# Rounding pass of an int8-quantised FFN on Trainium2: two elementwise adds moved from VectorE to ScalarE

## The chip, the cores and the metric

The kernel runs on all 8 cores of one Trainium2 chip. Each core computes one of the 8 sequences (2048 tokens, 1024 features); the cores exchange nothing. The metric is the device time of the slowest core in microseconds (us). Engines in the profile: PE is TensorE, DVE is VectorE, ACT is ScalarE, POOL is GpSimd, SP is SyncE.

## What is computed

For each sequence `x` of shape 2048 x 1024 the reference does an attention layer whose weights are `1 + s + s*s/2` in place of an exponential, and then a linear layer on activations quantised to int8 for each token:

```python
x = layernorm(x + attention(x, Wq, Wk, Wv, Wo))
# ffn
amax    = max(|x|, axis=-1)
x_scale = maximum(amax, 1e-6) / 127
x_q     = clip(round(x / x_scale), -128, 127).astype(int8)
acc     = x_q @ weight_q.T                    # exact integers
x = layernorm(x + acc * x_scale * weight_scale + bias)
```

The part that matters here is `x_q`: one rounding of 2048 x 1024 values to the nearest integer on each core, ties to even.

## The kernel before

Every instruction is written by hand into one of five streams (`plan.op("vector", ...)`, `"scalar"`, `"gpsimd"`, `"tensor"`, `"sync"`). An engine works through its own stream in the order in which the source emits it. Between engines, and between dependent instructions of the same engine, the order is kept by counting semaphores: `sDV` for VectorE, `sSc` for ScalarE, `sPE` for TensorE, `sPo` for GpSimd, `sIO` and `sCa` for transfers. `waits=[(sDV, sDV.n)]` means "wait until everything that was counted on VectorE up to here is done". Each wait is an instruction of its own ahead of the one that it guards, and a wait that this stream has already made is left out.

The stages follow each other: the projections to q, k and v; the attention, pair of heads by pair; the output projection with the first residual (`mkr1`, L605, with sums of squares on ScalarE, `mksq1`, L612, and a maximum and minimum on VectorE, L617 and L620); a run of small operations on 128x16 statistics (L625 to L662); the **rounding pass**; the int8 linear layer (L797) with its own residual (L808, L815, L824); statistics again (from L834); and the output rows, scaled on VectorE (L855) and stored (L861).

The rounding pass is one loop over `NT = 16` tiles of 128 tokens x 1024 features. Tile `t` uses buffers `t6[t % 2]` (f32) and `xq32[t % 2]` (int32); `er` is another name for `t6`, and `g32` is the same memory again, seen as int32. In the order of the VectorE stream the steps of a tile are:

- `mk1` (L705): `t6 = x1 * S2 + MM2`, the scaled value. Completion is what `mkxm` on GpSimd waits for.
- `mkc` (L712): `xq32 = int(t6)`, a cast.
- `mke` (L716): `t6 = t6 - xq32`, the remainder, a two-input operation.
- `mkm1` (L720): `t6 = t6 + MAGIC`, and `mkm2` (L724): `t6 = t6 - MAGIC`, with `MAGIC = 12582912.0`. Together they round the remainder to a multiple of one.
- `mkg` (L728): `g32 = int(2 * t6)`.
- `mk2b` (L735): `xq = xq32 + g32`, the rounded value as f16. It also waits for the transposes of tile `t-2`.

Beside it, for each tile, GpSimd scales the residual (`mkxm`, L741, one input) and adds the bias (`mkx1b`, L756, two inputs), both in place on `x1`. TensorE transposes `xq` in 8 blocks (L766) once `mk2b` is done, and ScalarE copies the result from PSUM into `xqT` (`mktre`, L776). In source order ScalarE's instruction for tile `t` is this copy and nothing else. TensorE's stream has all 128 transposes ahead of the first matmul of the linear layer, so that layer starts when tile 15 has been transposed.

Of the kernel before, what the change touches and what calls it, by code (L numbers as in the profile page):

```python
# [10 lines left out]
AF = mybir.ActivationFunctionType  # L11
ALU = mybir.AluOpType
# [15 lines left out]
MAGIC = 12582912.0  # L28
# [76 lines left out]
def _build_nc_inner(debug, _waits, collect_only=False):  # L105
# [34 lines left out]
    sSc = Sem(e(nc.semaphore("sSc")), "sSc")  # L140
    sDV = Sem(e(nc.semaphore("sDV")), "sDV")
# [44 lines left out]
    plan = Plan(nc, last_wait)  # L186
    plan.future_waits = _waits

    for dst, src in ((wsb, d_wsb), (biasb, d_biasb), (tri, d_tri),
                     (ident, d_ident), (ones2, d_ones2)):  # L190
        plan.op("sync", lambda sy, dst=dst, src=src: sy.dma_start(dst[:, :], src),
                incs=[(sIO, 16)])
# [8 lines left out]
    for fi in range(NCH):  # L201
# [3 lines left out]
                incs=[(sCa, 16)])  # L205
# [3 lines left out]
                incs=[(sCa, 16)])  # L209
# [9 lines left out]
    for proj in range(2):  # L219
        for c in range(NCH):  # L220
# [6 lines left out]
            for fi in range(NCH):  # L227
                waits = [(sCa, dma_after[(proj, fi)])]
                if prev in evac_dv:
                    waits.append((sDV, evac_dv[prev]))  # L230
                for qcc in range(QC):
# [5 lines left out]
                    incs = ()  # L237
                    if qcc == QC - 1 and (c == NCH - 1 or fi == NCH - 1):
                        incs = [(sPE, 1)]
                    plan.op("tensor", mk, waits=waits if qcc == 0 else (),  # L240
                            incs=incs)
# [5 lines left out]
            def mkev(v, ps=ps, dst=dst, scale=scale, c=c):  # L247
# [3 lines left out]
                    incs=[(sDV, 1)])  # L251
            evac_dv[(proj, c)] = sDV.n
        nxt = d_wkt if proj == 0 else d_wvt
        for fi in range(NCH):
# [4 lines left out]
                    waits=[(sPE, w_last_use[(proj, fi)])],  # L259
                    incs=[(sCa, 16)])  # L260
# [8 lines left out]
           for i in range(2)]  # L269

    plan.op("vector", lambda v: v.memset(vz_blocks[:, :, 64:65], 1.0),
            incs=[(sDV, 1)])

    v_evac = {}
    for t in range(NT):
# [6 lines left out]
        for fi in range(NCH):  # L282
            waits = [(sCa, dma_after[(2, fi)])] + extra
            extra = []
            for half in range(2):
# [5 lines left out]
                incs = [(sPE, 1)] if (fi == NCH - 1 and half == 1) else ()  # L291
                plan.op("tensor", mk, waits=waits if half == 0 else (), incs=incs)
                waits = ()
# [9 lines left out]
    if debug:  # L303
        plan.op("sync", lambda sy: sy.dma_start(d_qto, qT[:, :]),
                waits=[(sDV, n_qk_evac)], incs=[(sIO, 16)])
        plan.op("sync", lambda sy: sy.dma_start(d_kto, kT[:, :]),
                waits=[(sDV, n_qk_evac)], incs=[(sIO, 16)])
        plan.op("sync", lambda sy: sy.dma_start(d_vzo, vz[:, :]),
                waits=[(sDV, n_vz_done)], incs=[(sIO, 16)])
# [18 lines left out]
    for fi in range(NCH):  # L328
# [4 lines left out]
                incs=[(sCa, 16)])  # L333
# [80 lines left out]
    for p in range(NP):  # L414
# [128 lines left out]
        if p > 0:  # L543
# [3 lines left out]
                waits=wio, incs=[(sIO, 16)])  # L547
        gather_done[p] = sIO.n
        if debug and p == 0:
            plan.op("sync", lambda sy: sy.dma_start(d_oso, ot_sb[0][:, :]),  # L550
                    incs=[(sIO, 16)])
# [20 lines left out]
    if debug:  # L572
        plan.op("sync", lambda sy: sy.dma_start(d_oto, ot_fin[:, :]),
                waits=list(w_all), incs=[(sIO, 16)])

    r1_done = {}
    for t in range(NT):
        wio = []
        if t >= 2:
            wio.append((sDV, r1_done[t - 2]))  # L580
        plan.op("sync",
                lambda sy, t=t: sy.dma_start(xstream[t % 2][:, :],
                                             d_xtok[t * 128:(t + 1) * 128, :]),
                waits=wio, incs=[(sIO, 16)])
# [7 lines left out]
        for fi in range(NCH):  # L592
            for half in range(2):
# [5 lines left out]
                incs = [(sPE, 1)] if (fi == NCH - 1 and half == 1) else ()  # L599
# [11 lines left out]
        def mksq1(s, t=t):  # L611
# [3 lines left out]
                incs=[(sSc, 1)])  # L615
# [3 lines left out]
        def mkmn(v, t=t):  # L619
# [6 lines left out]
            waits=[(sDV, r1_done[NT - 1])], incs=[(sDV, 1)])  # L626
    plan.op("vector", lambda v: v.tensor_scalar(V1, SQ1, INV1024, None, ALU.mult),
            waits=[(sSc, n_sq1)], incs=[(sDV, 1)])
    plan.op("vector", lambda v: v.tensor_tensor(MSQ, M1, M1, ALU.mult),
            waits=[(sDV, sDV.n)], incs=[(sDV, 1)])  # L630
    plan.op("vector", lambda v: v.tensor_tensor(V1, V1, MSQ, ALU.subtract),
            waits=[(sDV, sDV.n)], incs=[(sDV, 1)])
    plan.op("scalar", lambda s: s.activation(V1, V1, AF.Sqrt, bias=c_eps),
            waits=[(sDV, sDV.n)], incs=[(sSc, 1)])
    plan.op("vector", lambda v: v.reciprocal(V1, V1),
            waits=[(sSc, sSc.n)], incs=[(sDV, 1)])
# [3 lines left out]
            waits=[(sDV, n_rstd1)], incs=[(sDV, 1)])  # L640
    plan.op("vector", lambda v: v.tensor_tensor(MN, M1, MN, ALU.subtract),
            waits=[(sDV, sDV.n)], incs=[(sDV, 1)])
    plan.op("vector", lambda v: v.tensor_tensor(MX, MX, MN, ALU.max),
            waits=[(sDV, sDV.n)], incs=[(sDV, 1)])
    plan.op("vector", lambda v: v.tensor_tensor(AM, MX, V1, ALU.mult),
            waits=[(sDV, sDV.n)], incs=[(sDV, 1)])
    plan.op("vector",
            lambda v: v.tensor_scalar(XS, AM, 1e-6, INV127, ALU.max, ALU.mult),
            waits=[(sDV, sDV.n)], incs=[(sDV, 1)])
    plan.op("vector", lambda v: v.reciprocal(RQ, XS),  # L650
            waits=[(sDV, sDV.n)], incs=[(sDV, 1)])
# [24 lines left out]
    er = t6  # L676
# [23 lines left out]
    for t in range(NT):  # L700
# [10 lines left out]
        def mkc(v, t=t):  # L711
            return v.tensor_copy(xq32[t % 2][:, :], t6[t % 2][:, :])  # L712
        plan.op("vector", mkc, waits=[(sDV, rnd1_done[t]), (sDV, sDV.n)],
                incs=[(sDV, 1)])
# [1 line left out]
            return v.tensor_tensor(t6[t % 2][:, :], t6[t % 2][:, :],  # L716
                                   xq32[t % 2][:, :], ALU.subtract)
        plan.op("vector", mke, waits=[(sDV, sDV.n)], incs=[(sDV, 1)])
        def mkm1(v, t=t):
            return v.tensor_scalar(er[t % 2][:, :], er[t % 2][:, :],  # L720
                                   MAGIC, None, ALU.add)
        plan.op("vector", mkm1, waits=[(sDV, sDV.n)], incs=[(sDV, 1)])
        def mkm2(v, t=t):
            return v.tensor_scalar(er[t % 2][:, :], er[t % 2][:, :],  # L724
                                   -MAGIC, None, ALU.add)
        plan.op("vector", mkm2, waits=[(sDV, sDV.n)], incs=[(sDV, 1)])
        def mkg(v, t=t):
            return v.tensor_scalar(g32[t % 2], er[t % 2][:, :],  # L728
                                   2.0, None, ALU.mult)
        plan.op("vector", mkg, waits=[(sDV, sDV.n)], incs=[(sDV, 1)])  # L730
        wv = [(sDV, sDV.n)]
        if t >= 2:
            wv.append((sPE, tr_done[t - 2]))
# [186 lines left out]
```

How the kernel before makes its waits and increments, by code:

```python
        def thunk(eng, wl=wl, builder=builder, incs=tuple(incs)):  # L74
            for s, v in wl:
                eng.wait_ge(s.h, v)
            inst = builder(eng)
            for s, k in incs:
                inst = inst.then_inc(s.h, k)
```

## Time and profile before

| | us |
|---|---|
| time before, median of 2 runs | 1013.87 (1012.25 to 1015.49) |
| time of the profiled execution | 1014.62 |
| its span, slowest core (core 4) | 1013.1 |
| spans of the 8 cores | 1006.6 to 1013.1 |
| VectorE busy | 543.4 (54%) |
| ScalarE busy | 375.7 (37%) |
| TensorE matmul busy | 617.9 (61%) |
| GpSimd busy | 110.8 (11%) |

The span runs from the first to the last instruction of a core. All times of rows are from core 4 and from that one profiled execution. Busy shares are averages over stages with different limits, so a stage is read by itself: the rounding pass lies between about 756 and 907 us of the span.

### The profile page before, as it was taken

To read this page: it belongs to the slowest core of one execution; us is meant where nothing else is said; L and a number is where in the kernel's file an instruction comes from. 1 tells how busy PE (TensorE), PEld (TensorE's weight loads), DVE (VectorE), ACT (ScalarE), POOL (GpSimd) and SP (SyncE) were. 2 spreads that over 40 slices of the span, in tenths; PEclk is the share of its full clock that TensorE was granted. 3 is DMA by queue.
4 is the path that set the end of the run, shared out by engine and by line. 5 is a ranking of instruction groups with operands and counts; after the bars stand their busy time and mean duration, and the time that the engine had idled before them with its cause. 6 is when DMAs were issued, how large, how long until landed. Compare 5 with 4: busy or idle time off the path is not lost.

```text
span 1013.1 us, 8858 instructions; the slowest of 8 cores (1006.6 to 1013.1 us)
## 1 busy us (share of the span) xinstructions
PE 617.9 (61%) x2688; PEld 222.6 (22%) x2688; DVE 543.4 (54%) x825; ACT 375.7 (37%) x403; POOL 110.8 (11%) x100
## 2 busy tenths in 40 slices
PE   1259859839977877877877778709941011029910
PEld 0014314304412222222222222203410000014400
DVE  0003202303345666556566656535989999976742
ACT  0000000000089879788879888801320110112310
POOL 1100000020000000000000000001014554530000
PEclk9999959959989889799979988858975555559965
DMA  6640230145000011011010111116410000000025
GB/s 107 115 70 1 32 52 1 27 59 82 1 1 1 23 32 38 18 42 33 21 33 22 33 32 23 31 44 199 164 63 0 0 1 0 0 1 1 1 111 221
DMA packets 14833, 43.89 MB, mean 43 GB/s; under 512 B 2244, under 2 KB 2756, under 8 KB 13764
## 3 DMA queue, kind: packets, MB, share of 16 engines
q0 software_dynamic: 8192, 23.07, 12.0%
q1 hardware_dynamic: 6596, 20.25, 6.0%
q8 instruction: 24, 0.39, 0.2%
q14 instruction: 21, 0.17, 0.1%
HBM read 44.11 MB, written 8.52 MB: 52 GB/s over the span
## 4 chain that ended last, share of the span: by engine, by line
PE 31%; DVE 22%; DMA 22%; ACT 14%; issue 9%; POOL 0%; DVEq 0%; ACTq 0%; POOLq 0%; SPq 0%
ACT uab L462 14%; PE pq L235 9%; PE oab L505 7%; DMA xs<-x_tok 6%; PE pa L797 6%; DMA wbuf<-wqt 6%; PE pv L289 5%; DVE t L720 4%; PE ps L442 4%; DVE t L716 3%; DMA wbuf<-wvt 3%; DMA wbuf<-wkt 3%; DVE xq L735 2%; DVE uab L470 2%; DVE ot_fin L375 2%
## 5 line engine op out<-in xcount | busy, mean ns | idle before, releaser
L462 ACT ACTIVATE uab<-ps,consts 128x1024 f16<-128x1024 f32 (+1 forms) x320 | 320.8, 1080 | 56.2 <-PE ps L442 56.1
L505 PE MATMUL oab<-uab,vz 128*65 128x512 f16 (+3 forms) x640 | 194.5, 389 | 62.4 <-DVE uab L485 31.6
L235 PE MATMUL pq<-xTsb,wbuf 128*128 128x512 f16 x512 | 128.4, 414 | 69.0 <-DMA wbuf<-wqt 53.7
L442 PE MATMUL ps<-qT,kT 64*128 64x512 f16 (+3 forms) x640 | 124.8, 387 | 22.9 <-ACT uab L462 21.0
L485 DVE TENSOR_SCALAR uab<-uab 128x1024 f16<-128x1024 f16 x192 | 79.4, 422 | 105.0 <-ACT uab L462 105.0
L462 ACT ACT_TABLE_LOAD x1 | 1.3, 1283 | 281.1 <-PE ps L442 281.1
L766 PE MATMUL pt<-ident_sb,xq 128*128 128x128 f16 x128 | 16.2, 306 | 146.4 <-DVE xq L735 146.4
L235 PEld LDWEIGHTS pq<-xTsb,wbuf 128*128 128x128 f16 x512 | 51.7, 103 | 145.2 <-issue 94.2
L505 PEld LDWEIGHTS oab<-uab,vz 128*65 128x65 f16 x640 | 48.2, 116 | 144.3 <-issue 143.3
L470 DVE SCALAR_TENSOR_TENSOR uab<-uab,tri_sb 128x256 f16<-128x256 f16 x128 | 54.5, 426 | 42.9 <-ACT uab L462 41.3
L597 PE MATMUL py<-woT,ot_fin 128*128 128x512 f16 x256 | 59.2, 388 | 25.9 <-DMA ot_fin<-ob_tmp 25.4
L289 PE MATMUL pv<-wbuf,xTsb 128*128 128x512 f16 x256 | 61.0, 400 | 20.7 <-DMA wbuf<-wvt 18.2
L248 DVE TENSOR_SCALAR qT<-pq 128x2048 f16<-128x2048 f32 x8 | 18.3, 2292 | 101.7 <-PE pq L235 101.7
L442 PEld LDWEIGHTS ps<-qT,kT 64*128 64x128 f16 x640 | 35.0, 94 | 154.1 <-issue 153.4
L776 ACT COPY xqT<-pt 128x1024 f16<-128x1024 f16 x16 | 16.2, 1012 | 140.6 <-PE pt L766 140.6
L797 PE MATMUL pa<-wqf,xqT 128*128 128x512 f16 x256 | 57.5, 388 | 0.0
L298 DVE CAST vz<-pv 128x1024 f16<-128x1024 f32 x16 | 19.6, 1225 | 59.9 <-PE pv L289 59.9
L248 DVE TENSOR_SCALAR kT<-pq 128x2048 f16<-128x2048 f32 x8 | 18.3, 2292 | 60.2 <-PE pq L235 60.2
L756 POOL TENSOR_TENSOR x<-x,biasb_sb 128x1024 f32<-128x1024 f32 x16 | 49.9, 3119 | 2.4
L766 PEld LDWEIGHTS pt<-ident_sb,xq 128*128 128x128 f16 x128 | 12.4, 137 | 150.5 <-issue 150.5
L612 ACT ACTIVATE scratch<-x 128x1024 f32<-128x1024 f32 x16 | 16.9, 1057 | 72.3 <-DVE x L605 72.3
L720 DVE TENSOR_SCALAR t<-t 128x1024 f32<-128x1024 f32 x16 | 42.3, 2643 | 1.7
(67 smaller groups left out, 491.9 us busy)
## 6 DMA issues: line engine op xcount, KB each, us to landing
rzb<-rzscr POOLq DMA_DIRECT2D x16, 512.0 KB, 4.6
xs<-x_tok SPq DMA_DIRECT2D x16, 512.0 KB
xTsb<-xT POOLq DMA_DIRECT2D x8, 512.0 KB, 5.6
out<-xs SPq DMA_DIRECT2D x8, 512.0 KB
out<-t SPq DMA_DIRECT2D x8, 512.0 KB
wbuf<-wqt POOLq DMA_DIRECT2D x8, 256.0 KB, 6.3
wbuf<-wkt POOLq DMA_DIRECT2D x8, 256.0 KB, 3.5
wbuf<-wvt POOLq DMA_DIRECT2D x8, 256.0 KB, 3.5
```

The source lines that it names most:

```text
L235: return t.matmul(ps[:, qcc * 512:(qcc + 1) * 512], lhs, rhs, start=(fi == 0), stop=(fi == NCH - 1))
L248: return v.tensor_scalar(dst[:, c * T:(c + 1) * T], ps[:, :], scale, None, ALU.mult)
L289: return tt.matmul(ps[:, half * 512:(half + 1) * 512], lhs, rhs, start=(fi == 0), stop=(fi == NCH - 1))
L442: return t.matmul(ps[:, ab * 512 + js: ab * 512 + 512], lhs, rhs, start=True, stop=True, tile_position=(r0, 0))
L462: return s.activation(dst, src, AF.Square, bias=c_rs, scale=c_rs)
L470: return v.scalar_tensor_tensor(ub[:, :, js:js + 128], ub[:, :, js:js + 128], 0.5, tri[:, None, :].broadcast_to([128, 2, 128]), ALU.add, A ...
L485: return v.tensor_scalar(ub[:, :, :], ub[:, :, :], 0.5, None, ALU.add)
L505: return t.matmul(ob[0:65, ab * 512 + js: ab * 512 + 512], lhs, rhs, start=(kt == 0), stop=(kt == 4 * qc + 3))
L597: return tt.matmul(ps[:, half * 512:(half + 1) * 512], lhs, rhs, start=(fi == 0), stop=(fi == NCH - 1))
L720: return v.tensor_scalar(er[t % 2][:, :], er[t % 2][:, :], MAGIC, None, ALU.add)
L756: return g.tensor_tensor(x1[:, t * D:(t + 1) * D], x1[:, t * D:(t + 1) * D], biasb[:, :], ALU.add)
L797: return tt.matmul(ps[:, half * 512:(half + 1) * 512], lhs, rhs, start=(fi == 0), stop=(fi == NCH - 1))
```

## The change

The two additions `mkm1` and `mkm2` leave the VectorE stream and enter the ScalarE stream, as activations with the function Copy, a scale of one and the constant as bias. Their places in the source stay between `mke` and `mkg`. `mkm1` now waits for VectorE's `mke` and for everything counted on ScalarE; `mkm2` waits for `mkm1` on ScalarE's own semaphore; and `mkg`, still on VectorE, waits for `mkm2` through ScalarE's semaphore. Everything else keeps its engine and its order.

```diff
-        def mkm1(v, t=t):
-            return v.tensor_scalar(er[t % 2][:, :], er[t % 2][:, :],
-                                   MAGIC, None, ALU.add)
-        plan.op("vector", mkm1, waits=[(sDV, sDV.n)], incs=[(sDV, 1)])
-        def mkm2(v, t=t):
-            return v.tensor_scalar(er[t % 2][:, :], er[t % 2][:, :],
-                                   -MAGIC, None, ALU.add)
-        plan.op("vector", mkm2, waits=[(sDV, sDV.n)], incs=[(sDV, 1)])
+        def mkm1(s, t=t):
+            return s.activation(er[t % 2][:, :], er[t % 2][:, :], AF.Copy,
+                                bias=MAGIC)
+        plan.op("scalar", mkm1, waits=[(sDV, sDV.n), (sSc, sSc.n)],
+                incs=[(sSc, 1)])
+        def mkm2(s, t=t):
+            return s.activation(er[t % 2][:, :], er[t % 2][:, :], AF.Copy,
+                                bias=-MAGIC)
+        plan.op("scalar", mkm2, waits=[(sSc, sSc.n)], incs=[(sSc, 1)])
         def mkg(v, t=t):
             return v.tensor_scalar(g32[t % 2], er[t % 2][:, :],
                                    2.0, None, ALU.mult)
-        plan.op("vector", mkg, waits=[(sDV, sDV.n)], incs=[(sDV, 1)])
+        plan.op("vector", mkg, waits=[(sSc, sSc.n)], incs=[(sDV, 1)])
```

## Rows read from the trace of the kernel before

**Rows 1.** Page, part 2: the span in 40 slices, busy tenths of each engine
```profile
PE   1259859839977877877877778709941011029910
DVE  0003202303345666556566656535989999976742
ACT  0000000000089879788879888801320110112310
POOL 1100000020000000000000000001014554530000
```

**Rows 2.** Chain of waits, 720 to 1014 us: start us, us, what
```profile
755.78 0.19 DVE stat L662
...
756.07 0.82 DVE t L705
...
907.08 1.01 PE pt L766 x8
908.10 57.27 PE pa L797 x256
```

**Rows 3.** Timeline of the fifth tile; tile 15's copy: start us, us, engine, line, operation, idle before it
```profile
792.41 1.23 DVE L735 TENSOR_TENSOR xq<-xq,t 128x1024 f16<-128x1024 int32 x1 [0.17 <-DVE t L728]
793.56 0.81 DVE L705 TENSOR_SCALAR t<-x,stat 128x1024 f32<-128x1024 f32 x1
793.89 1.01 PE L766 MATMUL pt<-ident_sb,xq 128*128 128x128 f16 x8 [8.39 <-DVE xq L735]
794.54 1.69 POOL L741 TENSOR_SCALAR x<-x,stat 128x1024 f32<-128x1024 f32 x1 [4.45 <-DVE t L705]
794.99 1.01 ACT L776 COPY xqT<-pt 128x1024 f16<-128x1024 f16 x1 [8.39 <-PE pt L766]
795.26 2.03 DVE L716 TENSOR_TENSOR t<-t,xq 128x1024 f32<-128x1024 f32 x1
796.37 3.12 POOL L756 TENSOR_TENSOR x<-x,biasb_sb 128x1024 f32<-128x1024 f32 x1
797.40 2.65 DVE L720 TENSOR_SCALAR t<-t 128x1024 f32<-128x1024 f32 x1
800.15 0.69 DVE L724 TENSOR_SCALAR t<-t 128x1024 f32<-128x1024 f32 x1
800.95 0.69 DVE L728 TENSOR_SCALAR t<-t 128x1024 int32<-128x1024 f32 x1
801.82 1.23 DVE L735 TENSOR_TENSOR xq<-xq,t 128x1024 f16<-128x1024 int32 x1 [0.17 <-DVE t L728]
802.96 0.81 DVE L705 TENSOR_SCALAR t<-x,stat 128x1024 f32<-128x1024 f32 x1
...
908.19 1.01 ACT L776 COPY xqT<-pt 128x1024 f16<-128x1024 f16 x1 [8.39 <-PE pt L766]
```

**Rows 4.** Groups by line and shape, 750 to 910 us: count, busy us, mean ns
```profile
L756 POOL TENSOR_TENSOR x<-x,biasb_sb 128x1024 f32<-128x1024 f32 x16 | 49.9, 3119 | 2.4
L720 DVE TENSOR_SCALAR t<-t 128x1024 f32<-128x1024 f32 x16 | 42.3, 2643 | 1.7
L735 DVE TENSOR_TENSOR xq<-xq,t 128x1024 f16<-128x1024 int32 x16 | 19.6, 1226 | 3.0 <-DVE t L728 2.8
L724 DVE TENSOR_SCALAR t<-t 128x1024 f32<-128x1024 f32 x16 | 11.1, 694 | 1.7
```

**Rows 5.** Groups of ScalarE by line and shape, whole span, columns as in rows 4
```profile
L462 ACT ACTIVATE uab<-ps,consts 128x1024 f16<-128x1024 f32 x224 | 252.9, 1207 | 44.8 <-PE ps L442 44.8
L612 ACT ACTIVATE scratch<-x 128x1024 f32<-128x1024 f32 x16 | 16.9, 1057 | 72.3 <-DVE x L605 72.3
L776 ACT COPY xqT<-pt 128x1024 f16<-128x1024 f16 x16 | 16.2, 1012 | 140.6 <-PE pt L766 140.6
L462 ACT ACT_TABLE_LOAD x1 | 1.3, 1283 | 281.1 <-PE ps L442 281.1
```

**Rows 6.** Timeline, handovers between VectorE and ScalarE around the statistics, columns as in rows 3
```profile
751.87 0.17 DVE L631 TENSOR_TENSOR stat<-stat 128x16 f32<-128x16 f32 x1
752.14 0.31 ACT L633 ACTIVATE stat<-stat,consts 128x16 f32<-128x16 f32 x1 [1.96 <-DVE stat L631]
752.55 0.25 DVE L635 RECIPROCAL stat<-stat 128x16 f32<-128x16 f32 x1 [0.50 <-ACT stat L633]
...
968.07 0.08 DVE L815 DVE_READ_ACCUMULATOR x<-t,x 128x1 f32 x1
...
968.31 1.06 ACT L824 ACTIVATE scratch<-x 128x1024 f32<-128x1024 f32 x1 [2.30 <-DVE x L815]
```

## Prediction

> **What bounds the kernel now.** I read the page's 40 slices first, to see which engine is full where [rows 1]. One slice is 25.3 us. From slice 30 (about 760 us) to slice 35 VectorE shows 9 tenths while TensorE shows 0 or 1, ScalarE 0 or 1 and GpSimd 4 or 5. That is the rounding pass, and there VectorE looks like the limit. Full is not the same as limiting, so the chain of waits comes next [rows 2]: it runs on VectorE alone from the last statistic (755.78) through the first L705 (756.07) up to tile 15, and then passes to TensorE, to the eight transposes at 907.08 and the 256 matmuls of the linear layer, 57.27 us long. TensorE takes its stream in order, so every microsecond that the 16 tiles of the rounding pass lose or gain arrives undiminished at 908.10. The matmuls last as long as before, whenever they begin.
>
> Then the timeline of one tile [rows 3]. The reader is to see three things in it. First, the period: L705 starts at 793.56 and again at 802.96, so a tile takes 9.40 us, and the seven VectorE steps follow one another without a gap worth naming. Second, L720 takes 2.65 us and L724, the same addition on the same buffer with the same shape, 0.69. Over the 16 tiles the means are 2643 and 694 ns [rows 4]. So 1.95 us of L720 are not its own. Third, who is running then: GpSimd's L756 ends at 796.37 + 3.12 = 799.49, and L720 ends at 800.05, 0.56 us later, about the time that one such addition needs. I read it thus: L720 was issued at 797.40 while L756 was at work, could not move until L756 was done at 799.49, and then ran at its usual speed. The step before looks alike: L716 starts at 795.26, GpSimd's L741 ends at 794.54 + 1.69 = 796.23, and L716 ends at 797.29, 1.06 later. L716's two-input relative L735 takes 1226 ns [rows 4], not 2.03. The two engines take turns. What is on the path of a tile is in part GpSimd's work.
>
> The Trainium skill has a rule for this pair: on the page "SBUF — State Buffer", section "Who interferes with whom", it says that VectorE and GpSimd share one pair of ports under a lock held for a whole instruction, the loser blocking fully, and that ScalarE never waits on anyone. The 0.56 us from L756's end to L720's end agree with the first half. For the second, ScalarE's copy L776 lies wholly beside GpSimd's L741 here (794.99 to 796.00 in 794.54 to 796.23) and takes the 1.01 us that it also takes for tile 15, at 908.19, long after GpSimd's last step [rows 3]; so the trace agrees, as far as a copy that reads PSUM and writes SBUF can show it.
>
> **The change part by part.** The stretch that changes reaches from L716's end to L728's start. Before: 797.29 to 800.95, that is 3.66 us: a gap of 0.11, L720 with 2.65, a gap of 0.10, L724 with 0.69, a gap of 0.11 [rows 3].
>
> What comes in its place, term by term:
>
> - VectorE to ScalarE. L633 starts 0.10 after L631's end (751.87 + 0.17 = 752.04, to 752.14). But `mkm1` has two waits, as L824 has, and L824 starts 0.16 after the end of what it waits for (968.07 + 0.08 = 968.15, to 968.31) [rows 6]. I take 0.16. The second wait, on ScalarE's own count, is long met: the copy L776 of the tile before ends at 794.99 + 1.01 = 796.00, 1.29 us before L716's end [rows 3].
> - `mkm1` on ScalarE. No row shows a Copy activation with f32 in SBUF on both sides. The nearest is L612, an activation of 128x1024 f32 from SBUF to SBUF, at 1057 ns; it bounds nothing by itself, so I take the copy L776 at 1012 below and L462, which reads scale and bias from memory, at 1207 above [rows 5]. The value is that of L612, the row with the same shape, type and memories: 1.06.
> - ScalarE to itself. No row shows ScalarE waiting for its own last result. VectorE does that in 0.11 (L716 to L720). Below it is the 0.10 of a handover, above it the 0.25 between L735 of the tile before (792.41 + 1.23 = 793.64) and its transposes (793.89), the longest handover in these rows [rows 3]. I take 0.11.
> - `mkm2`: the same 1.06.
> - ScalarE to VectorE: L633 ends at 752.45 and L635 starts at 752.55, 0.10 [rows 6].
>
> Sum: 0.16 + 1.06 + 0.11 + 1.06 + 0.10 = 2.49 us. The stretch shrinks by 3.66 - 2.49 = 1.17 us a tile.
>
> L728 keeps its 0.69 only if GpSimd is out of the way when it is issued, since it is a VectorE step of the kind that L720 was. GpSimd is released by L705, not by anything moved, and L756 ended 799.49 - 797.29 = 2.20 us after L716. L728 now starts 2.49 after it, 0.29 us past that end. So the wait on GpSimd doesn't move to L728: it lies beside ScalarE's two additions. The cover is thin. Each 0.1 us that GpSimd is later than 0.29 is 0.1 us a tile back.
>
> What else sees the edit. ScalarE's copy L776 stands behind `mkm2` of its own tile and ahead of `mkm1` of the next. It is waiting for the transposes anyway, starts 1.10 us after these do and is done 1.29 us before L716 ends, so neither the copy nor the next `mkm1` is held. `mk1` of tile t+2 waits for `mk2b` of tile t, unchanged. GpSimd's 4.45 us of idle before L741 [rows 3] shrink to 3.28, so it stays off the path with its 4.8 us of work in a period of now 8.23. VectorE's wait for `mkm2` blocks what is queued behind it, L728, L735 and the next tile's L705; they are in the sum, since the whole period is counted. The linear layer, statistics and stores are untouched and simply begin earlier.
>
> Total: 16 x 1.17 = 18.7 us. Against the profiled execution's own 1014.62 that is 995.9. The median of the runs shown lies 0.75 below that execution, so I forecast **995 us**, 1.9% faster. About 2% is what a measurement of this kernel can tell from no change. That bound is at 0.98 x 1013.87 = 993.6, hard by the forecast, which makes "within 2%" the likelier word, and not by far.
>
> **The rivals.** *ScalarE is cheaper* than L612. With 1.01 for each activation (L776's row) and 0.10 for each of the three handovers a stretch is 2.32 and the gain 1.34 x 16 = 21.4: 992.4. The floor under it is GpSimd: L728 can't end before L756's end plus 0.56, at 800.05, against 801.64 now, 1.59 us a tile, 25.4 in all, 988.4. For it: a copy has less to do than a square with a sum. Against: L612 has the exact operands.
>
> *ScalarE is dearer.* With 1.21 each (L462's row) and 0.25 for each handover the stretch is 3.17, the gain 0.49 x 16 = 7.8, 1006; with only the activations at 1.21 it is 2.79, the gain 13.9, 1000. For it: ScalarE's own-result wait is unseen. Against: L462 reads PSUM and two operands more.
>
> *The stall only changes its victim, and the kernel gets slower.* If L756 can't finish until VectorE leaves it room, or is later than its span tells, L728 is stretched to 2.65 as L720 was. The tile then takes 2.49 + 2.65 = 5.14 from L716's end to L728's end, against 801.64 - 797.29 = 4.35: 0.79 more, 12.6 us in all, 1026. It decides from the point where L756 ends 1.59 us later than it does. For it: the margin is 0.29 us, and spans of GpSimd are rough. Against: L756 and L720 have the same lengths in this tile as in the mean of all 16 (3.12 and 3119 ns, 2.65 and 2643) [rows 3, 4], so their order never slips, and nothing new is put in L756's way. The same sign follows when L720's surplus is ignored: two activations at 1.06 against two additions at 0.69. The Trainium skill says just that on "ScalarE: Activation LUTs", section "Rules for kernel authors": additions belong on VectorE, not on ScalarE. The rows agree with its prices (694 ns against 1057); that it gives the wrong sign here hangs on L720's 2643.
>
> *Copy and the copy or the square need different tables.* A table load is 1283 ns [rows 5]. One a tile on the path gives 1.17 - 1.28 = -0.11, 1015.6; two give 22 us more, 1036. Against: only one load stands in the whole span, though a square, the copy L776 and a square root (L633) all ran. A single load more would cost 1.3.
>
> **How the numbers follow.** Forecast as worked out, 992.5 to 999: 0.70. ScalarE cheaper: 0.12. Dearer: 0.11. The stall moves: 0.05. Tables: 0.02. The range should leave out no more than 2 in 10: from 991, inside the cheap case, to 1000, where only the activations are dear. Faster by over 2% (under 993.6): the cheap case with 0.12, and 0.13 of the forecast's own, because the two runs shown lie 3 us apart and the bound 1.4 below my number; 0.25. Slower by over 2% (over 1034): only two table loads a tile, 0.02. Within 2%: 0.73.
>
> **What would show it.** In the timeline of the changed kernel a tile's period should be 8.2 us; two ScalarE activations of 1.06 should stand between L716's end and the L728 step, which should start 2.5 us after L716's end and keep 0.69; L716 should still take 2.03 and L756 3.12; the transposes of tile 15 should start near 888 and the 57.3 us of matmuls behind them be the same. No new table load should be there. I am wrong if `mkg` is longer than 0.7 us (the stall has moved), if an activation takes over 1.2 us, if the gap between the two is over 0.2 us, or if the linear layer begins some 19 us earlier and the end does not.

## The result

The changed kernel takes **994.35 us** (median of 11 runs) against 1013.88 for the kernel before (median of 10 runs beside them). The ratio is 0.9796 with a 95% interval of 0.9771 to 0.982, that is 2.0% faster, on the border of what can be told from no change. The forecast was 995. In some executions the cores of one die show a lower granted clock and the time is some per cent longer (one of the 11 here, at 1029.99 us); medians take in all runs, ratios only the undisturbed ones.

All rows of a kernel are from its slowest core, for the changed kernel core 5. The chain of waits of the changed kernel, late in the span, shows the same structure as before [rows 2], but with ScalarE in it: the second addition (now L725 on ScalarE), the doubling (L729), the last rounding step (L736), the transposes, the matmuls. Columns are start us, us, what.

```profile
884.96 1.06 ACT t L725
...
886.12 0.71 DVE t L729
...
886.99 1.24 DVE xq L736
...
888.47 1.01 PE pt L767 x8
```

The timeline of one tile of the changed kernel, the fourth, answers [rows 3]:

```profile
782.41 1.69 POOL L742 TENSOR_SCALAR x<-x,stat 128x1024 f32<-128x1024 f32 x1 [3.25 <-DVE t L705]
782.87 1.01 ACT L777 COPY xqT<-pt 128x1024 f16<-128x1024 f16 x1 [3.56 <-PE pt L767]
783.14 2.03 DVE L716 TENSOR_TENSOR t<-t,xq 128x1024 f32<-128x1024 f32 x1
784.25 3.13 POOL L757 TENSOR_TENSOR x<-x,biasb_sb 128x1024 f32<-128x1024 f32 x1
785.32 1.06 ACT L720 ACTIVATE t<-t 128x1024 f32<-128x1024 f32 x1 [1.43 <-DVE t L716]
786.47 1.06 ACT L725 ACTIVATE t<-t 128x1024 f32<-128x1024 f32 x1
787.63 0.69 DVE L729 TENSOR_SCALAR t<-t 128x1024 int32<-128x1024 f32 x1 [2.46 <-ACT t L725]
788.49 1.23 DVE L736 TENSOR_TENSOR xq<-xq,t 128x1024 f16<-128x1024 int32 x1 [0.17 <-DVE t L729]
```

The reader is to see that nothing but the two additions changed. The subtraction L716 is still 2.03 us and GpSimd's bias add (L757) still 3.13. Both activations take 1.06 while that bias add is running. VectorE is idle for 2.46 us before L729, which then takes its plain 0.69. GpSimd is done at 784.25 + 3.13 = 787.38, and L729 starts at 787.63, 0.25 us later.

To compare kernels I use one table, read from the trace of every core. The period is the mean distance of the L705 steps. The pass is the time from the first L705 to the first matmul of the linear layer; the linear layer is counted from there to the start of its last matmul, and the rest from that start to the end of the span. All are medians over the 8 cores of the profiled execution, in us:

```
kernel                         before pass   period    pass    linear layer   rest     span
before                              753.15     9.42   151.85          56.85   48.25   1009.95
changed                             753.10     8.20   132.30          57.30   47.15    989.15
e1 before, no GpSimd step           754.00     6.66   107.75          56.70   47.85    967.00
e2 changed, no GpSimd step          753.75     7.39   119.40          56.65   47.35    977.10
e3 first addition moved             752.55     8.60   138.70          56.70   47.35    995.20
e4 second addition moved            750.45     9.80   157.90          56.95   47.10   1012.30
e5 changed, GpSimd longer           751.15    10.11   162.80          56.75   46.85   1017.65
e6 before, bias adds late           748.75     7.47   128.40          57.00   47.85    982.35
e7 changed, bias adds late          752.30     8.20   136.10          56.35   47.10    993.35
e8 short rounding                   752.65     3.13    51.20          56.55   48.35    908.30
e9 bias adds late and gated         756.05     7.47   120.65          56.90   48.30    982.35
e10 scaling on ScalarE              753.85     6.66   107.70          56.50   47.95    966.55
e11 as e5, other form               751.20     9.15   147.60          56.55   47.00   1002.20
e12 correction by 4096              752.40     9.42   151.80          56.90   48.25   1009.15
```

The pass is the same to 0.1 us on all 8 cores of a kernel. The stages ahead of it differ by 5 to 15 us between the cores of one execution, whichever the kernel, and in the traces that is most of what sets the slowest core apart. So the pass is the sharp measure here and the total the blunt one. The change took 19.55 us out of the pass.

### The profile page after: what moved, and what is told of

Its sections match the earlier page's. It is cut to its first block, busy times and chain, and to the rows that moved or that the text cites. A ratio compares the mean times of both kernels' runs of the same rounds, so it can differ in the third digit from the quotient of the medians.

```text
span 993.9 us, 8874 instructions; the slowest of 8 cores (981.0 to 993.9 us)
## 1 busy us (share of the span) xinstructions
PE 614.4 (62%) x2688; PEld 222.0 (22%) x2688; DVE 490.0 (49%) x793; ACT 409.2 (41%) x435; POOL 111.2 (11%) x100
## 4 chain that ended last, share of the span: by engine, by line
PE 32%; DMA 22%; ACT 18%; DVE 17%; issue 9%; POOL 0%; DVEq 0%; ACTq 0%; POOLq 0%; SPq 0%
ACT uab L462 15%; PE pq L235 10%; PE oab L505 7%; PE pa L798 6%; DMA xs<-x_tok 6%; DMA wbuf<-wqt 6%; PE pv L289 6%; PE ps L442 4%; DVE t L716 3%; DMA wbuf<-wvt 3%; DMA wbuf<-wkt 3%; DVE xq L736 2%; DVE ot_fin L375 2%; DVE uab L470 2%; ACT t L720 2%
## 5 line engine op out<-in xcount | busy, mean ns | idle before, releaser
L505 PE MATMUL oab<-uab,vz 128*65 128x512 f16 (+3 forms) x640 | 191.7, 384 | 63.4 <-DVE uab L485 32.3
L757 POOL TENSOR_TENSOR x<-x,biasb_sb 128x1024 f32<-128x1024 f32 x16 | 50.0, 3127 | 2.4
L612 ACT ACTIVATE scratch<-x 128x1024 f32<-128x1024 f32 x16 | 16.9, 1057 | 73.7 <-DVE x L605 73.7
L524 DVE COPY otsb<-oab 65x1024 f32<-65x1024 f32 x32 | 38.8, 1213 | 4.2 <-PE oab L505 4.2
L777 ACT COPY xqT<-pt 128x1024 f16<-128x1024 f16 x16 | 16.2, 1012 | 56.6 <-PE pt L767 56.6
```

Source lines behind the costliest of these rows:

```text
L505: return t.matmul(ob[0:65, ab * 512 + js: ab * 512 + 512], lhs, rhs, start=(kt == 0), stop=(kt == 4 * qc + 3))
L524: return v.tensor_copy(dst, src)
L757: return g.tensor_tensor(x1[:, t * D:(t + 1) * D], x1[:, t * D:(t + 1) * D], biasb[:, :], ALU.add)
```

## The experiments

Two claims of the prediction carry it: that L720's 2.65 us were mostly a wait for GpSimd, and that the gain is this wait, filled with other work, and not the relief of VectorE. The rivals are that L720 is long by itself (theory B), and that VectorE's load is what counts (theory C). The first four kernels ran on one chip, beside a kernel before of 1016.65 us; e5 to e8 stood beside one of 1017.01, and e9 to e12 beside one of 1016.27.

### No GpSimd step in the pass

The edit, in the kernel before (e1) and in the changed one (e2), leaves the residual unscaled and without its bias:

```diff
-        plan.op("gpsimd", mkxm, waits=[(sDV, rnd1_done[t])], incs=[(sPo, 1)])
...
-        plan.op("gpsimd", mkx1b, waits=wx1b, incs=[(sPo, 1)])
-        x1b_done[t] = sPo.n
+        x1b_done[t] = 0
```

> The kernel before without GpSimd's two steps on x1 in the rounding pass (the residual is then neither scaled nor given its bias, so that part of the result is left out). Theory A, turns with GpSimd: the first addition loses its surplus of 1.95 us (2.65 to 0.69) and the subtraction before it its 0.80 (2.03 to 1.23); a tile takes 6.65 us in place of 9.40, the kernel 970. Theory B, the first addition is long by itself (it follows a two-input step): it stays at 2.65, the tile at 9.40, the kernel at 1014. Theory C, only VectorE's load counts: nothing on VectorE was removed, 1014.

Measured: 972.87 us (2 runs), ratio 0.9558 (0.9486 to 0.9629). First the group of the subtraction in the kernel before, 750 to 910 us (its neighbours are in [rows 4]), then two groups of e1, 750 to 872 us:

```profile
L716 DVE TENSOR_TENSOR t<-t,xq 128x1024 f32<-128x1024 f32 x16 | 32.5, 2031 | 1.7
```

```profile
L716 DVE TENSOR_TENSOR t<-t,xq 128x1024 f32<-128x1024 f32 x16 | 19.6, 1225 | 1.7
L720 DVE TENSOR_SCALAR t<-t 128x1024 f32<-128x1024 f32 x16 | 11.1, 695 | 1.7
```

Not one VectorE instruction was edited, and the first addition went from 2643 to 695 ns, the subtraction from 2031 to 1225. The period is 6.66, expected 6.65. Theories B and C are both out: what made these two steps long was another engine's work.

> The changed kernel without GpSimd's two steps on x1 (the same part of the result is left out). Theory A: only the subtraction gets shorter, by 0.80 us, since the activations never met GpSimd; a tile takes 7.41 in place of 8.21, the kernel 982, and that is 12 us MORE than the kernel before without the same steps: the sign of the change turns. Theories B and C: 994, 20 below the other.

Measured: 984.46 us (2 runs), ratio 0.9672 (0.9608 to 0.9735); the period is 7.39, expected 7.41. The row of this pair is in the table: without GpSimd the pass takes 107.75 us with the additions on VectorE and 119.40 with them on ScalarE. The very change that won 19.55 us loses 11.65 once there is no wait to fill. This is the case that the Trainium skill describes on "ScalarE: Activation LUTs", section "Rules for kernel authors" (additions on VectorE): it holds in e1 and e2, and it gives the wrong sign in the kernel as it stands, since it prices the instruction and not the wait in front of it. The factor of up to about 3 that the section gives is for bf16; in f32 the rows here show 1057 against 694 ns, a factor of 1.5, so what they confirm is the direction.

### One addition at a time

e3 moves `mkm1` and leaves `mkm2` on VectorE, e4 the reverse:

```diff
 e3, in the changed kernel
-        def mkm2(s, t=t):
-            return s.activation(er[t % 2][:, :], er[t % 2][:, :], AF.Copy,
-                                bias=-MAGIC)
-        plan.op("scalar", mkm2, waits=[(sSc, sSc.n)], incs=[(sSc, 1)])
+        def mkm2(v, t=t):
+            return v.tensor_scalar(er[t % 2][:, :], er[t % 2][:, :],
+                                   -MAGIC, None, ALU.add)
+        plan.op("vector", mkm2, waits=[(sSc, sSc.n)], incs=[(sDV, 1)])
...
-        plan.op("vector", mkg, waits=[(sSc, sSc.n)], incs=[(sDV, 1)])
+        plan.op("vector", mkg, waits=[(sDV, sDV.n)], incs=[(sDV, 1)])
```

> Only the first addition on ScalarE, the second stays on VectorE. Theory A: the second addition is issued 1.31 us after the subtraction's end, has to wait until GpSimd's bias add is done at 2.20 and ends at 2.76 (it shows 1.45 us); the next step starts at 2.87 in place of 3.66; a tile takes 8.61, the kernel 1001. Theory B: 2.65 us are replaced by 1.06 and the second addition keeps 0.69; a tile takes 7.85, the kernel 989, faster than with both moved. Theory C: two thirds or more of the gain, by VectorE's busy time relieved.

Measured: 1004.27 us (4 runs), ratio 0.9866 (0.9793 to 0.9939), period 8.60, expected 8.61. The timeline of one tile of e3:

```profile
783.25 3.12 POOL L757 TENSOR_TENSOR x<-x,biasb_sb 128x1024 f32<-128x1024 f32 x1
784.32 1.06 ACT L720 ACTIVATE t<-t 128x1024 f32<-128x1024 f32 x1 [1.43 <-DVE t L716]
785.49 1.44 DVE L725 TENSOR_SCALAR t<-t 128x1024 f32<-128x1024 f32 x1 [1.31 <-ACT t L720]
787.03 0.69 DVE L729 TENSOR_SCALAR t<-t 128x1024 int32<-128x1024 f32 x1
```

The stall has a new victim. L725, an addition that took 0.69 in all 16 tiles before, takes 1.44, because it now is the one to meet the bias add: that ends at 786.37, L725 at 786.93, again 0.56 later. The expectation said 1.45.

> Only the second addition on ScalarE, the first stays on VectorE. Theories A and B: the first addition keeps 2.65 us and 0.69 is replaced by 1.06 and a longer handover; the next step starts 4.07 us after the subtraction's end in place of 3.66; a tile takes 9.81, the kernel 1020, slower than before. Theory C: VectorE is relieved of 0.69 us a tile, 11 us, 1003.

Measured: 1024.11 us (10 runs), ratio 1.0041 (1.0005 to 1.0076); the period is 9.80, expected 9.81, and the pass 6.05 us longer than before. In one tile of e4 the first addition waits as before, and ScalarE's addition comes behind it:

```profile
778.99 2.64 DVE L720 TENSOR_SCALAR t<-t 128x1024 f32<-128x1024 f32 x1
781.78 1.06 ACT L724 ACTIVATE t<-t 128x1024 f32<-128x1024 f32 x1 [4.29 <-DVE t L720]
782.94 0.69 DVE L728 TENSOR_SCALAR t<-t 128x1024 int32<-128x1024 f32 x1 [1.31 <-ACT t L724]
```

Moving 0.69 us of work a tile off the engine that shows 90% busy made the pass longer, and the whole kernel about 0.4%. So theory C is out a second time, and the change decomposes: by the table the first addition alone brings 13.15 us of the pass, the second alone costs 6.05, and both together bring 19.55. The second pays only behind the first, where VectorE would otherwise still be waiting for GpSimd.

### How thin the cover is

The prediction put GpSimd's bias add 0.29 us ahead of L729. e5 makes GpSimd later, by one more step between its two. The step writes a buffer that the first VectorE step of the linear layer uses, so that step is also made to wait for the last bias add (the linear layer keeps its length, 56.75 us in the table):

```diff
+        def mkex(g, t=t):
+            return g.tensor_scalar(t3[0][:, :], biasb[:, :], 1.0, None, ALU.mult)
+        plan.op("gpsimd", mkex, waits=[(sPo, sPo.n), (sIO, n_const)],
+                incs=[(sPo, 1)])
...
-        wv = [(sPE, n_acc), (sIO, n_const)]
+        wv = [(sPE, n_acc), (sIO, n_const), (sPo, x1b_done[NT - 1])]
```

> The changed kernel with one more GpSimd step (a one-input scaling of 128x1024 into a buffer that is free then) between the residual's scaling and its bias add. Theory A with the thin cover of the prediction: GpSimd is done 3.27 us after the subtraction's end in place of 2.20, so the step behind the two activations, issued at 2.46, is stretched from 0.69 to about 1.4; a tile takes 8.9 us in place of 8.21, the kernel 1005. Rival, ScalarE alone sets the pace of the changed kernel: 994, the step keeps 0.69.

Measured: 1023.62 us (5 runs), ratio to before 1.0079 (1.0052 to 1.0105), period 10.11. The whole gain is gone and more, far past the 1005 that I expected, so the expectation missed. One tile of e5 shows why:

```profile
776.71 2.03 DVE L716 TENSOR_TENSOR t<-t,xq 128x1024 f32<-128x1024 f32 x1
777.83 3.54 POOL L748 TENSOR_SCALAR t<-biasb_sb 128x1024 f32<-128x1024 f32 x1 [0.16 <-POOL x L742]
...
781.20 0.71 DVE L729 TENSOR_SCALAR t<-t 128x1024 int32<-128x1024 f32 x1 [2.46 <-ACT t L725]
781.52 2.59 POOL L761 TENSOR_TENSOR x<-x,biasb_sb 128x1024 f32<-128x1024 f32 x1
782.09 3.10 DVE L736 TENSOR_TENSOR xq<-xq,t 128x1024 f16<-128x1024 int32 x1 [0.17 <-DVE t L729]
```

The added step took from L716's end (778.74) to 781.37, 2.63 us and not the 1.07 that I had read off its neighbour L742. L729, issued at 781.20, slipped in ahead of the bias add, which then ran from L729's end (781.91) to 784.11, its usual 2.20. The victim was the two-input step L736, at 3.10 in place of 1.23. e11 gives the added step the form of its neighbour, with scale and offset read from memory:

```diff
-            return g.tensor_scalar(t3[0][:, :], biasb[:, :], 1.0, None, ALU.mult)
+            return g.tensor_scalar(t3[0][:, :], biasb[:, :],
+                                   V1[:, t:t + 1], NMR[:, t:t + 1],
+                                   ALU.mult, ALU.add)
```

> As e5, with the added GpSimd step in the very form of its neighbour (scale and offset from memory in place of an immediate 1.0). If the 2.63 us that the added step held the turn in e5 are the form's, it is 1.07 here: the step behind the activations is then stretched to about 1.4 us, a tile takes 8.9, the kernel 1005, as e5 was expected to be. If they are the length of any step that follows another one, 10.11 a tile and 1023 as in e5.

Measured: 1010.13 us (8 runs), ratio 0.9944 (0.9919 to 0.9969), period 9.15. The same rows of e11:

```profile
782.88 2.03 DVE L716 TENSOR_TENSOR t<-t,xq 128x1024 f32<-128x1024 f32 x1
784.01 1.97 POOL L748 TENSOR_SCALAR t<-biasb_sb,stat 128x1024 f32<-128x1024 f32 x1 [0.17 <-POOL x L742]
...
786.13 2.34 POOL L763 TENSOR_TENSOR x<-x,biasb_sb 128x1024 f32<-128x1024 f32 x1
...
787.37 1.65 DVE L729 TENSOR_SCALAR t<-t 128x1024 int32<-128x1024 f32 x1 [2.46 <-ACT t L725]
```

Now the added step holds the turn from 784.91 to 785.98, 1.07 us, and L729 is the victim with 1.65, ending 0.55 after the bias add's end (788.47). The period is 0.25 above the 8.9 expected: GpSimd needs 0.15 to go from the one step to the next and 2.34 for a bias add that it starts with nobody ahead of it, which the estimate had at nothing and 2.20. GpSimd's last step of a tile now ends 788.47 - 784.91 = 3.56 us after the subtraction, in place of 787.38 - 785.17 = 2.21 in the changed kernel. That is 1.35 later, and the tile is 0.95 longer: the first 0.4 were free, the 0.25 of the cover and a little more, and the remainder was paid in full. So the changed kernel sits near the edge.

### Taking the cause away

If the wait for GpSimd is the cause, moving GpSimd's work is the better cure. The bias adds are needed by the linear layer's residual step (L815) only. e6 puts them behind the loop in GpSimd's stream, with both additions back on VectorE (lines behind the first step shift by one: L721, L725 and L729 are the additions and the doubling); e7 does it in the changed kernel:

```diff
-        plan.op("gpsimd", mkx1b, waits=wx1b, incs=[(sPo, 1)])
-        x1b_done[t] = sPo.n
+        late.append((mkx1b, n_xm))
...
+    for t, (bld, n_xm) in enumerate(late):
+        plan.op("gpsimd", bld, waits=[n_xm, (sIO, n_const)], incs=[(sPo, 1)])
+        x1b_done[t] = sPo.n
```

> The kernel before with GpSimd's 16 bias adds behind the rounding loop in GpSimd's stream, beside the linear layer. Same result, both additions on VectorE. Theory A: the first addition shrinks from 2.65 to 0.69, a tile takes 7.45 us, the kernel 983, and up to 990 if the bias adds take turns with VectorE's residual step of the linear layer; faster than the change itself. Theories B and C: 1014.

Measured: 990.82 us (6 runs), ratio 0.9747 (0.9711 to 0.9783), period 7.47, expected 7.45. The pass is 128.40 long, though, nearly 8 us more than 16 such periods and the last tile's transposes ask for. The timeline of VectorE in tile 15 of e6 shows where they are, and GpSimd's row beside it who held it:

```profile
876.82 2.64 DVE L721 TENSOR_SCALAR t<-t 128x1024 f32<-128x1024 f32 x1
879.57 2.64 DVE L725 TENSOR_SCALAR t<-t 128x1024 f32<-128x1024 f32 x1
882.32 2.64 DVE L729 TENSOR_SCALAR t<-t 128x1024 int32<-128x1024 f32 x1
885.13 3.10 DVE L736 TENSOR_TENSOR xq<-xq,t 128x1024 f16<-128x1024 int32 x1 [0.17 <-DVE t L729]
```

```profile
875.62 48.21 POOL L757 TENSOR_TENSOR x<-x,biasb_sb 128x1024 f32<-128x1024 f32 x16
```

The queue of bias adds begins as soon as the last L742 is done, inside tile 15, and the last four VectorE steps of that tile each lose a turn: three times 2.64 for 0.69 and once 3.10 for 1.23, together 7.7 us (the expectation of e9, below, says five steps; the subtraction keeps its 2.03).

> The changed kernel with the same 16 bias adds behind the loop. Theory A: in the changed kernel they are hidden behind the activations, so a tile stays at 8.21 us and the kernel at 994, or a few us more. Rival, the two gains add up: 983 - 19 = 964.

Measured: 998.3 us (4 runs), ratio 0.9827 (0.9796 to 0.9858), period 8.20 as in the changed kernel, pass 3.8 us longer through the same tile 15 (two steps there lose a turn, the doubling and the last one). The gains do not add: the change and the late bias adds remove the same wait. e9 also lets the first bias add wait for tile 15:

```diff
-        plan.op("gpsimd", bld, waits=[n_xm, (sIO, n_const)], incs=[(sPo, 1)])
+        plan.op("gpsimd", bld, waits=[n_xm, (sIO, n_const),
+                                      (sDV, rnd2_done[NT - 1])],
+                incs=[(sPo, 1)])
```

> As e6 (both additions on VectorE, bias adds behind the loop), but the first bias add waits for the last rounding step of tile 15. In e6 the bias adds began inside tile 15 and stretched its last five VectorE steps, some 8 us (rounding pass 128.4 us at 7.47 a tile). Theory A: the pass takes 120.5 us in place of 151.8, the linear layer stays at 57, the kernel 983 by the medians (ratio 0.969). Rival, the late bias adds cost the linear layer what they spare the pass: e6's time or more.

Measured: 986.98 us (5 runs), ratio 0.9695 (0.9647 to 0.9744). The pass is 120.65, expected 120.5. The linear layer stays at 56.90 though the bias adds now run beside it. Its rows show the price and who pays it:

```profile
879.14 29.11 POOL L757 TENSOR_TENSOR x<-x,biasb_sb 128x1024 f32<-128x1024 f32 x10 [5.31 <-DVE xq L736]
...
889.42 1.27 DVE L814 SCALAR_TENSOR_TENSOR t<-pa,stat,wsb_sb 128x1024 f32<-128x1024 f32 x1
...
890.87 1.93 DVE L821 SCALAR_TENSOR_TENSOR x<-t,x 128x1024 f32<-128x1024 f32 x1 [0.17 <-DVE t L814]
```

The residual step L821 (L815 before) takes 1.93 in place of its 1.23 in this tile and in most of those in which GpSimd is busy (3.39 in one of them). With 1.93 a tile of VectorE's is 3.3 us long there (889.42 to 892.73), and TensorE's 57 us for 16 tiles are 3.6. The waits have moved to a stage where TensorE's work covers them.

e10 moves the last GpSimd step of the pass too, the scaling of the residual, to ScalarE:

```diff
-        def mkxm(g, t=t):
-            return g.tensor_scalar(x1[:, t * D:(t + 1) * D],
-                                   x1[:, t * D:(t + 1) * D],
-                                   V1[:, t:t + 1], NMR[:, t:t + 1],
-                                   ALU.mult, ALU.add)
-        plan.op("gpsimd", mkxm, waits=[(sDV, rnd1_done[t])], incs=[(sPo, 1)])
+        def mkxm(s, t=t):
+            return s.activation(x1[:, t * D:(t + 1) * D],
+                                x1[:, t * D:(t + 1) * D], AF.Identity,
+                                bias=NMR[:, t:t + 1], scale=V1[:, t:t + 1])
+        plan.op("scalar", mkxm, waits=[(sDV, rnd1_done[t])], incs=[(sSc, 1)])
```

> As e9, and the scaling of the residual moved from GpSimd to ScalarE (an activation with scale and bias from memory), so that no GpSimd step lies in the rounding pass. Same computation as before. Theory A: like e1 without leaving anything out: the subtraction shrinks from 2.03 to 1.23 us, a tile takes 6.66, the pass 107.8, the kernel 970 (ratio 0.957). Rival, ScalarE's 1.2 us activation and its copy take over as the pace or meet VectorE in memory: 7.47 a tile or more, 983.

Measured: **973.03 us** (4 runs), ratio 0.9565 (0.952 to 0.9611), period 6.66, pass 107.70, the same as e1 with nothing left out. One tile of e10:

```profile
782.22 1.23 DVE L717 TENSOR_TENSOR t<-t,xq 128x1024 f32<-128x1024 f32 x1
782.86 1.24 ACT L742 ACTIVATE x<-x,stat 128x1024 f32<-128x1024 f32 x1
783.55 0.69 DVE L721 TENSOR_SCALAR t<-t 128x1024 f32<-128x1024 f32 x1
784.35 0.69 DVE L725 TENSOR_SCALAR t<-t 128x1024 f32<-128x1024 f32 x1
```

ScalarE's activation lies across two VectorE steps, and both keep the 1.23 and 0.69 us that they take in e1. This is the second half of the rule that the prediction took from the Trainium skill, "SBUF — State Buffer", section "Who interferes with whom" (ScalarE waits on nobody, VectorE and GpSimd take turns on a shared pair of ports). The trace agrees here for an activation that reads and writes SBUF, at 1.24 us beside a VectorE step of 1.23, and in the changed kernel at 1.06 (1056 to 1058 ns in all 32) beside a GpSimd step. The ports themselves no trace shows.

### The arithmetic of the pass

> The kernel before with the factor of the correction 4096 in place of 2. If the remainder ever rounds to something but zero, the quantised values move by 4096 steps there and the output with them; if the cast rounds to nearest, the correction is zero everywhere, nothing moves, and e8 leaves out nothing but work. Time unchanged, 1014, under either.

Measured: 1013.79 us (1 run), and the output is still that of the reference, where one correction other than zero would have moved a value by thousands of steps. So on this input the remainder never rounds to anything but zero, and the subtraction, the two additions and the doubling work on a correction that is zero. e8 leaves these four steps out and keeps the bias adds late:

```diff
         def mk2b(v, t=t):
-            return v.tensor_tensor(xq[t % 2][:, :], xq32[t % 2][:, :],
-                                   g32[t % 2], ALU.add)
+            return v.tensor_copy(xq[t % 2][:, :], xq32[t % 2][:, :])
```

> Subtraction, both additions and the doubling left out (if the cast to int32 rounds to nearest, the remainder is at most 0.5 and the correction is always zero, so the result stays the same), the last step a plain copy from int32 to f16, and the bias adds behind the loop. Theory A: scaling 0.81, cast 0.69, then the copy waits for GpSimd's scaling of the residual (1.07) and takes about 1.65; a tile takes 3.2 us, the kernel about 915, to 925 if the bias adds delay the linear layer's residual step. Were the cast a truncation, the result would be off by whole steps of the quantiser.

Measured: **922.33 us** (4 runs), ratio 0.9044 (0.8976 to 0.9112), period 3.13, expected 3.2. One tile of e8, with the copy at 1.44 us because it waits its turn behind GpSimd's scaling:

```profile
778.00 1.69 POOL L725 TENSOR_SCALAR x<-x,stat 128x1024 f32<-128x1024 f32 x1 [1.44 <-DVE t L706]
778.79 1.44 DVE L720 CAST xq<-xq 128x1024 f16<-128x1024 int32 x1 [0.17 <-DVE xq L713]
```

The pass is down to 51.2 us on every core. The total lies above the expected 915 because on two cores, 4 and 5, the matmuls of the linear layer took 63.3 and 63.7 us in place of 56.5. On core 4 the granted clock, averaged over the stretch in which these run at first, was 0.80 of full speed, between the two levels of 1.2 and 2.4 GHz; on core 5 it was 0.79, on the other six cores 0.99 to 1.00, and in the same layer of the kernel before 1.00 from 912 us on. Stretches of core 4 of e8, columns as in the page's part on engines, then clock, DMA share, GB/s:

```profile
812.00:840.00 28.00, 28.00 (x107) 11.61 (x106) 21.26 (x18) 5.88 (x11) 28.00 (x11) 0.80 0.00 1
840.00:875.00 35.00, 33.10 (x146) 14.42 (x143) 26.28 (x29) 11.37 (x20) 14.21 (x5) 0.95 0.00 0
```

It wasn't one execution alone: in another of the four runs cores 6 and 7 are the long ones (918.8 and 919.0 us, mean clock 0.837 and 0.838, the other six at 0.850 to 0.855), and the run in which no core fell back took 911.10 us, below the 915. Whether the denser work of all engines makes this more frequent, no run here tells.

## Why the prediction was right, step by step

**The chain.** VectorE's pass sets the end, and what it gains arrives whole. Right: 19.55 us left the pass (table) and the linear layer stayed within 0.5 us. One reading on the way was off and nothing rests on it: VectorE shows 9 tenths in slices 30 to 34, and 7 in slice 35, where TensorE is at 2 and GpSimd at 3 [rows 1]. The transposes of tile 15 were foretold near 888 and stand at 888.47.

**The wait inside L720.** Right, and shown by e1 (2643 to 695 ns with no VectorE edit) and e3 (the stall appears in L725). That GpSimd and VectorE take turns whole instructions at a time is shown by the constant 0.55 to 0.56 us between a bias add's end and the end of the addition that waited for it, in before, e3 and e11. The rows that the prediction gave for ScalarE's independence were thinner than it says: L741 was issued at 794.54 but had its turn only from L712's end at 795.16, so the copy ran beside a working GpSimd for 0.84 of its 1.01 us. The changed kernel's activations, 1.06 us right across the bias add, settle it.

**The terms.** From the tile shown: handover with two waits 785.32 - 785.17 = 0.15 (0.16 foretold), activations 1.06 and 1.06 (1.06 each), ScalarE to itself 786.47 - 786.38 = 0.09 (0.11, and just under the 0.10 taken as its lower bound), ScalarE to VectorE 0.10 (0.10). Sum 2.46 against 2.49. The choice of L612 for a Copy activation, by shape, type and memory, hit to the nanosecond (1057). The range's outer bounds, 1012 and 1207, weren't needed.

**The size.** 1.17 us a tile was foretold, 1.20 are in the tile shown (3.66 - 2.46), 19.2 for 16. The last 0.35 comes from no term of the sum: L735 of the fifteenth tile had 0.52 us of idle ahead of it in the kernel before in place of 0.17, and it has not in the changed one.

The medians of the spans differ by 20.8. Beyond the pass that is mostly the stretch behind the linear layer, 48.25 and 47.15, and here the prediction was wrong in a small thing: it had the stores as untouched. One row of the kernel before and the same row of the changed one, both the sixth of the 16 output scalings on VectorE:

```profile
978.46 0.81 DVE L855 TENSOR_SCALAR xs<-x,stat 128x1024 f32<-128x1024 f32 x1 [2.83 <-DMA out<-xs]
```

```profile
959.52 0.81 DVE L856 TENSOR_SCALAR xs<-x,stat 128x1024 f32<-128x1024 f32 x1 [1.96 <-DMA out<-xs]
```

The wait for a store is 0.87 us shorter there. That isn't chance: each of the seven kernels without an addition on ScalarE (before, e1, e6, e8, e9, e10, e12) has one such wait of 2.8 to 3.1 us on all 8 cores, at this same place (in e1 at the fourteenth scaling), and each of the seven with one has none at that place. The rest is 47.85 to 48.35 us in the former and 46.85 to 47.35 in the latter. The 0.52 ahead of L735 goes the same way: it stands in the fifteenth tile of before, e1, e6, e9, e10 and e12 and in no other kernel. So some 1.2 us of what the edit brought is neither the wait for GpSimd nor in the sum, and its cause is open. That the forecast and the median lie only 0.65 us apart is therefore in part luck; the undisturbed runs of the changed kernel alone lie 8 us apart (989.81 to 997.99).

**The cover.** 0.29 us was foretold between the bias add's end and L729, 0.25 measured. Right as to place and size. "Each 0.1 us later is 0.1 us a tile back" was nearly right where L729 is the step that waits: in e11 GpSimd is 1.35 later and the tile 0.95 longer, where the rule gives 1.06. In e5 it doesn't hold: there the bias add ends 784.11 - 778.74 = 5.37 us after the subtraction, 3.16 later than in the changed kernel, and the tile is 1.91 longer, since L729 gets its turn ahead of the bias add. What failed besides was in the expectation of e5, not in the prediction: I took a GpSimd step's length from a neighbour of another form.

**The rivals.** The stall that only changes its victim happened in e3, e5 and e11, and in none of the changed kernel's tiles; in e3 and e11 it was the next VectorE step, in e5 the one after that. No table was loaded beyond the one. ScalarE was neither cheaper nor dearer than L612. The words "within 2%" were given the larger chance by 1.4 us, and the measured ratio lies right on that bound, with the interval on both sides of it.

## What to carry to other kernels

Where an instruction is several times longer than its twin on the same engine, with the same operation and shape, suspect a wait: look which other engine ends just before it does, and make the test by taking that engine's work away. The twin must have the same form: the added GpSimd steps of e5 and e11 have one shape, and one is 2.5 times longer by itself. Moving work to a slower engine pays when it fills a wait (19.55 us here), costs when there is none (11.65 us in e2 against e1), and is a cure of the symptom: moving the instructions that cause the wait gained more than twice as much (44.15 us of the pass in e10). Before tuning where a step runs, ask whether it changes the result at all (e12 and e8).

## What the hardware did that I hadn't expected

- The profile counts a blocked instruction as busy from its issue. VectorE looked 9 tenths busy in the pass of the kernel before; 2.76 us of each 9.42 (by the period of e1) were waiting. The same holds for GpSimd: L756's 3.12 us hold the turn for 2.20, L741's 1.69 for 1.07, which begin when VectorE's cast ends (794.47 + 0.69 = 795.16, by the row below) and last to 796.23 [rows 3].

```profile
794.47 0.69 DVE L712 CAST xq<-t 128x1024 int32<-128x1024 f32 x1
```

- A GpSimd scaling of 128x1024 f32 with an immediate and one operation held its turn for 2.63 us (e5), the same with two operations and both operands from memory for 1.07 (e11). Why, no run here tells.
- The same activation costs 1057 ns with immediates (L720, L725 of the changed kernel) and 1242 with scale and bias from memory (e10, where the function is Identity in place of Copy), 185 more. The Trainium skill, "ScalarE: Activation LUTs", section "What ACT_TABLE_LOAD costs", gives about 93 for each such operand; the trace agrees.
- A second wait ahead of an instruction, already met, costs about 0.07 us on VectorE: L736 of the changed kernel has one wait in the first two tiles, with 0.10 us of idle before it, and a second one, for transposes long done, in the other 14, with 0.17. On ScalarE, L720 has 0.15 with two waits, and on VectorE L729 has 0.10 with one.
